# Attention stage of a macaron block: three blocks' normalised rows and the payload's row numbers made on VectorE, and a payload ring of four buffers

## The chip, the cores and the metric

The kernel runs on one core of a Trainium2 chip. TensorE, VectorE, ScalarE, GpSimd and SyncE run their own instruction streams and meet at semaphores. The metric is the device time of one execution in microseconds (us).

## The reference

```python
x = L0_attn_batch                                   # 16 x 512 x 128, float32
x = x + 0.5 * ffn(layernorm(x), ...)                # mixture of 8 experts, 2 per token, and a shared one
x = x + attn(layernorm(x), Wq, bq, Wk, bk, Wv, bv, Wo, bo)
x = x + 0.5 * ffn(layernorm(x), ...)                # the same weights again
# ffn: scores = x @ router; the two best experts of each token, gate = sigmoid(score)
#      out = shared(x) + sum over both experts of (silu(g x @ w_in) * (g x @ w_swiglu)) @ w_out
# attn: softmax over each 128 keys of a sequence of 512 apart, the four results added and normalised
```

## The kernel before

The 8192 tokens are 16 blocks of four tiles of 128 rows. There are five stages: router and shared expert of the first feed-forward layer, its experts, attention, experts again, and an end that adds up. Between stages all engines meet.

**The attention stage** is the one that changes. Each block b goes through it in a hand-written software pipeline: every engine has a loop over i, and the names of helpers with i+3, i, i-2, i-3 tell how far ahead or behind a block is. The order on each engine is the order in the text, and only semaphores tie the engines together.
- SyncE loads the two expert results of each token into `Y2`, two blocks ahead.
- GpSimd adds the two (`total`, L968) and adds the sum to `X` (`added`, L973). It does this for eight blocks at the start, and for the other eight between the scatters of blocks 0 to 7. The scatter of a block (L992) is eight indirect DMAs that write rows of the payload `PAY` to DRAM at the rows in `POS`; their descriptors are made by GpSimd. A payload row is 128 values, the token's result row number (`AT_DEST`) and its gate (`AT_GATE`). Before the scatter GpSimd copies the row numbers (L980) and the second expert's 128 values (L982, in two halves).
- VectorE makes mean and variance (`moments_a`, L1020 and L1024), then, once ScalarE has the inverse deviation `RA`, the product `NA` = -mean x `RA` (`shift`, L1030). It also makes the maxima of the scores (`NM`, L1035), the weights and the scaling of the probabilities (L1058, twice a block, 128x1024), the update of `X` (L1064), the rescaled rows of the payload (`norm`, L1082), the choice of experts (`HOT`, `HOTB`), the gate (`gate`, L1094 and L1096) and the place of each row (`RANK`, `PICK`, `POS`).
- ScalarE makes `RA` (L1167, L1171), the normalised rows `AN` from `X`, `NA` and `RA` (`normalise`, L1178), copies between PSUM and SBUF, and the exponentials (L1215). In its loop `normalise(i + 3)` comes ahead of `exps(i + 1, 0)`.
- TensorE transposes `AN` (L1300), makes queries, keys, values, scores, the products with the values, and transposes the payload's rows once a block (`turn_kept`, L196) for the router.

`AB` is the number of buffers of `PAY` in this stage; block b uses `b % AB`, and `norm` waits for the scatter of block b - AB before it overwrites one.

Of the kernel before, what the change touches and what calls it, by code (L numbers as in the profile page):

```python
# [8 lines left out]
I32 = mybir.dt.int32  # L9
U32 = mybir.dt.uint32  # L10
ACT = mybir.ActivationFunctionType
ALU = mybir.AluOpType
# [3 lines left out]
BT = 4  # L16
# [23 lines left out]
def macaron(nc, batch, wq, bq, wk, bk, wv, bv, wo, bo, router, w_in_sh, w_out_sh, w_sw_sh,  # L40
# [23 lines left out]
    RB = 4  # L64
    AB = 3
    YBUFS = 4
# [11 lines left out]
    with ExitStack() as ctx:  # L78
        def sb(name, shape, dt=F32, mem=ctx):
            return mem.enter_context(nc.sbuf_tensor(name, shape, dt))  # L80
# [841 lines left out]
        with ExitStack() as mem, nc.Block() as block:  # L922
# [26 lines left out]
            KL = sb("KLa", [P, EARLY, W], F32R, mem=mem)  # L949
            SSG = sb("SSGa", [P, FC, W], mem=mem)  # L950
            EARLY_BANKS = ((4, 5), (0, 6))
            HID = Y2[:, :, :, :, :].rearrange("p b c j d -> p b (c j d)")
# [12 lines left out]
            def _(pool):  # L965
# [10 lines left out]
                def second(b, h):  # L976
                    half = slice(h * BT // 2, (h + 1) * BT // 2)
                    if h == 0:
                        pool.wait_ge(k["normed"], NB + b + 1)
                        pool.tensor_copy(PAY[:, b % AB, :, :, AT_DEST:AT_DEST + 1].bitcast(I32),  # L980
                                         dest[:, :, BT * b:BT * b + BT].unsqueeze(3))
                    pool.tensor_copy(PAY[:, b % AB, 1, half, 0:D], PAY[:, b % AB, 0, half, 0:D])\  # L982
                        .then_inc(k["pay2"], 1)
# [29 lines left out]
            def _(dve):  # L1013
# [13 lines left out]
                def shift(b):  # L1027

                    dve.wait_ge(k["a_rstd"], b + 1)
                    dve.scalar_tensor_tensor(out=NA[:, b % 4, :], in0=MA[:, b % 4, :, 0], scalar=-1.0, in1=RA[:, b % 4, :],  # L1030
                                             op0=ALU.mult, op1=ALU.mult).then_inc(k["a_shift"], 1)
# [60 lines left out]
                def gate(b):  # L1092
                    dve.wait_ge(k["gate_raw"], NB + b + 1)
                    st.did(dve.tensor_scalar(GE[:, b % 2, :, :], GE[:, b % 2, :, :], 1.0, None, ALU.add))  # L1094
                    st.settle()
                    dve.reciprocal(PAY[:, b % AB, :, :, AT_GATE:AT_GATE + 1],  # L1096
                                   GE[:, b % 2, :, :].rearrange("p j c -> p c j").unsqueeze(3)).then_inc(k["gated"], 1)
# [64 lines left out]
            def _(act):  # L1162
# [10 lines left out]
                def normalise(b):  # L1173
                    act.wait_ge(k["a_shift"], b + 1)
                    if b >= 2:
# [348 lines left out]
```

## Time and profile before

| | |
|---|---|
| three runs | 991.25 us median (988.44 to 995.65) |
| the profiled execution | 990.6 us, of which the profile's span is 988.9 us |
| attention's first sum on GpSimd | starts at 418.90 us |
| last sum of `X` on GpSimd (L973) | starts at 592.56 us |
| last scatter DMA issued by GpSimd (L992) | starts at 701.93 us, takes 0.96 us |
| last VectorE operation of attention | starts at 702.52 us, takes 0.69 us |
| first loads of the next stage on SyncE's queue | 707.45 us |
| busy over the span | PE 84%, DVE 65%, ACT 58%, POOL 65% |

Times in rows are from the start of the span. PE is TensorE, DVE VectorE, ACT ScalarE, POOL GpSimd, SP SyncE. A time stands for the whole stage only where the stage's rows say so; the shares over the span are means over stages with different limits.

### The profile page before, as it was taken

Reading aid. Unit: us, or ns where it says so; the run is one execution under the profiler, and the core shown is the slowest. Engines: PE = TensorE matmul, PEld = TensorE weight load, DVE = VectorE, ACT = ScalarE, POOL = GpSimd, SP = SyncE. Lnnn points to the kernel's source line nnn. Section 1 sums busy time; section 2 is a strip of 40 time slices with the busy share of each in tenths; the row PEclk is TensorE's granted clock in tenths of the full one; section 3 lists DMA queues with packets and bytes.
Section 4 is the critical chain, followed back from the end, with each engine's and each line's share of the span. In section 5 each row is a group of like instructions: output and inputs, shape, how many; then the busy total and the mean of one; then the engine's idle time right before and its main releaser. Section 6 shows DMA issues by size and latency. Waiting matters only on the chain. (4 is left out here: it accounts for less than half of the span.)

```text
span 988.9 us, 19495 instructions
## 1 busy us (share of the span) xinstructions
PE 835.5 (84%) x5857; PEld 732.3 (74%) x5857; DVE 644.2 (65%) x2022; ACT 573.3 (58%) x1662; POOL 647.2 (65%) x701
## 2 busy tenths in 40 slices
PE   4787777609999999369999999996599999994997
PEld 3676666509999999326776767775499999993886
DVE  6786654506666666157899998885366666661666
ACT  3324232117777777279988888862277777772332
POOL 4777777745777777470688887677367777774421
PEclk9797777959999999779999999996699999997999
DMA  9611111422333333250112211112423333333653
GB/s 233 189 47 44 44 46 43 85 70 71 104 106 102 109 107 102 74 150 22 49 59 75 79 39 40 36 44 63 88 80 103 109 106 109 101 97 109 170 153 105
DMA packets 112920, 88.01 MB, mean 89 GB/s; under 512 B 13426, under 2 KB 102132, under 8 KB 112820
## 3 DMA queue, kind: packets, MB, share of 16 engines
q1 hardware_dynamic: 94816, 51.08, 20.6%
q0 software_dynamic: 17280, 35.69, 10.8%
q8 instruction: 51, 0.84, 0.4%
q14 instruction: 49, 0.40, 0.1%
q10 hardware_dynamic: 724, 0.01, 0.0%
HBM read 43.68 MB, written 43.04 MB: 88 GB/s over the span
## 5 line engine op out<-in xcount | busy, mean ns | idle before, releaser
L820 POOL DMA_INDIRECT results<-YO,XS x284 | 275.6, 970 | 120.5 <-issue 84.7
L802 DVE TENSOR_TENSOR HT<-bank,SG 128x512 f32<-128x512 f32 x142 | 98.1, 691 | 132.9 <-PE bank L888 132.9
L886 PE MATMUL bank<-XSH,WX 128*128 128x256 f32 x568 | 174.1, 306 | 0.3 <-DVE WX L811 0.3
L992 POOL DMA_INDIRECT pairs<-PAY,POS x128 | 134.8, 1053 | 59.0 <-issue 28.8
L411 POOL DMA_INDIRECT pairs<-PAY,POS x128 | 128.3, 1002 | 57.8 <-issue 30.8
L887 PE MATMUL bank<-XSL,WX 128*128 128x256 f32 x568 | 162.0, 285 | 0.0
L888 PE MATMUL bank<-XSH,WX 128*128 128x256 f32 x568 | 161.9, 285 | 0.0
L904 PE MATMUL bank<-WOE,HT 128*128 x1136 | 150.2, 275 | 0.1
L904 PEld LDWEIGHTS bank<-WOE,HT 128*128 128x128 f32 x1136 | 138.1, 192 | 0.5 <-issue 0.5
L844 ACT ACTIVATE XG<-XS 128x128 f32<-128x128 f32 x284 | 111.0, 392 | 44.1 <-DMA XS<-pairs 44.1
L863 ACT ACTIVATE SG<-bank 128x512 f32<-128x512 f32 x142 | 84.9, 598 | 48.8 <-PE bank L888 48.8
L886 PEld LDWEIGHTS bank<-XSH,WX 128*128 128x128 f32 x568 | 110.2, 194 | 1.1 <-issue 1.1
L887 PEld LDWEIGHTS bank<-XSL,WX 128*128 128x128 f32 x568 | 110.7, 195 | 0.0
L888 PEld LDWEIGHTS bank<-XSH,WX 128*128 128x128 f32 x568 | 110.1, 194 | 0.0
L811 DVE CAST WX<-WE 128x1024 fp32r x142 | 97.4, 686 | 0.1
L1215 ACT ACTIVATE PR<-bank,NM 128x128 f32<-128x128 f32 x256 | 90.6, 378 | 1.0 <-DVE NM L1035 1.0
L894 PE MATMUL bank<-ident,XG 128*128 128x128 f32 x284 | 55.8, 279 | 35.0 <-ACT XG L844 35.0
L456 ACT ACTIVATE SSG<-bank 128x512 f32<-128x512 f32 x32 | 19.1, 595 | 113.7 <-PE bank L636 113.7
L808 DVE TENSOR_TENSOR XSL<-bank,XSH 128x256 fp32r<-128x256 f32 x142 | 58.7, 414 | 35.3 <-ACT XSH L849 35.2
L855 ACT ACTIVATE YO<-bank 128x256 f32<-128x256 f32 x142 | 54.7, 385 | 36.4 <-PE bank L904 36.4
L1363 PEld LDWEIGHTS bank<-V,PT 128*128 128x128 f32 x512 | 63.9, 197 | 6.7 <-issue 6.7
L1339 PE MATMUL bank<-KT,QT 128*128 128x512 f32 x128 | 65.7, 596 | 3.0 <-ACT PR L1215 2.5
(197 smaller groups left out, 1760.9 us busy)
## 6 DMA issues: line engine op xcount, KB each, us to landing
XS<-pairs SPq DMA_DIRECT2D x142, 130.0 KB, 2.3
Y<-results SPq DMA_DIRECT2D x32, 256.0 KB, 3.3
YF<-results SPq DMA_DIRECT2D x32, 256.0 KB, 3.4
results<-YO,XS POOLq DMA_INDIRECT x284
pairs<-PAY,POS POOLq DMA_INDIRECT x256, 2.3
out<-X SPq DMA_DIRECT2D x16, 256.0 KB, 2.5
pairs<-pad_rows SPq DMA_DIRECT2D x16, 130.0 KB
pairs<-pad_rows SPq DMA_DIRECT2D x1, 1040.0 KB, 15.3
```

What stands on the lines that cost most here:

```text
L411: pool.indirect_dma_start(pairs, bass.IndirectOffsetOnAxis(ap=POS[:, b % RB, j, c:c + 1], axis=0), PAY[:, b % RB, c, j, :], None).then_inc ...
L802: dve.tensor_tensor(HT[:, i % 2, :], bank[4 + i % 2][:, :], SG[:, i % 2, :], ALU.mult)\
L811: dve.tensor_copy(WX[:, i % 2, :, :].rearrange("p h f -> p (h f)"), WE[:, ds(e * 4 * F, 4 * F)]).then_inc(k["e_weights"], 1)
L820: pool.indirect_dma_start(results, bass.IndirectOffsetOnAxis(ap=XS[:, u, j, AT_DEST:AT_DEST + 1].bitcast(U32), axis=0), YO[:, u, j, :], No ...
L844: act.activation(XG[:, i % 2, j, :], XS[:, slot(i), j, 0:D], ACT.Copy, scale=XS[:, slot(i), j, AT_GATE:AT_GATE + 1]).then_inc(k["xs_scaled ...
L863: act.activation(SG[:, i % 2, :], bank[2 + i % 2][:, :], ACT.Silu).then_inc(k["e_silu"], 1)
L886: pe.matmul(ps, WX[:, i % 2, 1, w], hi, start=True, stop=False)
L887: pe.matmul(ps, WX[:, i % 2, 0, w], lo, start=False, stop=False)
L888: mm = pe.matmul(ps, WX[:, i % 2, 0, w], hi, start=False, stop=True)
L904: mm = pe.matmul(chunk(bank[6 + i % 2], j), HT[:, i % 2, (2 * c + j) * P:(2 * c + j + 1) * P], WOE[:, ds(e * FC * D + c * D, D)], start=(c ...
L992: pool.indirect_dma_start(pairs, bass.IndirectOffsetOnAxis(ap=POS[:, b % AB, j, c:c + 1], axis=0), PAY[:, b % AB, c, j, :], None).then_inc ...
L1215: ins = act.activation(PR[:, b % 2, a, g * P:(g + 1) * P], chunk(bank[4 + a % 2], g), ACT.Exp, bias=NM[:, b % 2, a, g:g + 1], accum_out=SU ...
```

## The change

`AB` goes from 3 to 4. For the first three blocks VectorE makes the normalised rows itself, in four instructions of one 128x128 tile each, in the place where it made `NA`; ScalarE leaves these three blocks out. The copy of the row numbers into the payload goes from GpSimd's `second` to VectorE's `gate`, in all 16 blocks.

```diff
-    AB = 3
+    AB = 4
...
+            FIRST = 3
...
                     if h == 0:
                         pool.wait_ge(k["normed"], NB + b + 1)
-                        pool.tensor_copy(PAY[:, b % AB, :, :, AT_DEST:AT_DEST + 1].bitcast(I32),
-                                         dest[:, :, BT * b:BT * b + BT].unsqueeze(3))
...
                 def shift(b):
-
                     dve.wait_ge(k["a_rstd"], b + 1)
+                    if b < FIRST:
+                        if b >= 2:
+                            dve.wait_ge(k["a_turned"], b - 1)
+                        for j in range(BT):
+                            ins = dve.tensor_scalar(AN[:, b % 2, j:j + 1, :], x_tile(b, j), MA[:, b % 4, j, 0:1],
+                                                    RA[:, b % 4, j:j + 1], ALU.subtract, ALU.mult)
+                        ins.then_inc(k["a_normed"], 1)
+                        return
...
                     st.settle()
+                    dve.tensor_copy(PAY[:, b % AB, :, :, AT_DEST:AT_DEST + 1].bitcast(I32),
+                                    dest[:, :, BT * b:BT * b + BT].unsqueeze(3))
                     dve.reciprocal(PAY[:, b % AB, :, :, AT_GATE:AT_GATE + 1],
...
                 def normalise(b):
-                    act.wait_ge(k["a_shift"], b + 1)
+                    if b < FIRST:
+                        return
+                    act.wait_ge(k["a_shift"], b + 1 - FIRST)
```

VectorE at the start of attention, before (`SA` and `MA` are the moments of a block, `NM` the first maximum of block 0's scores):

```order
L1020 BN_STATS SA<-X 128x6 x4
L1024 BN_AGGR MA<-SA 128x2 x4
L1030 SCALAR_TENSOR_TENSOR NA<-MA,RA 128x4
L1020 BN_STATS SA<-X 128x6 x4
L1024 BN_AGGR MA<-SA 128x2 x4
L1030 SCALAR_TENSOR_TENSOR NA<-MA,RA 128x4
L1020 BN_STATS SA<-X 128x6 x4
L1024 BN_AGGR MA<-SA 128x2 x4
L1030 SCALAR_TENSOR_TENSOR NA<-MA,RA 128x4
L1035 TENSOR_REDUCE NM<-bank 128x4
```

and now:

```order
L1019 BN_STATS SA<-X 128x6 x4
L1023 BN_AGGR MA<-SA 128x2 x4
L1032 TENSOR_SCALAR AN<-X,MA,RA 128x128 x4
L1019 BN_STATS SA<-X 128x6 x4
L1023 BN_AGGR MA<-SA 128x2 x4
L1032 TENSOR_SCALAR AN<-X,MA,RA 128x128 x4
L1019 BN_STATS SA<-X 128x6 x4
L1023 BN_AGGR MA<-SA 128x2 x4
L1032 TENSOR_SCALAR AN<-X,MA,RA 128x128 x4
L1041 TENSOR_REDUCE NM<-bank 128x4
```

Four instructions of a whole tile stand in the place of each product of 128x4, ahead of the next block's moments and of the first maximum.

GpSimd around the payload of the second block, before:

```order
L973 TENSOR_TENSOR X<-X,Y 128x512
L992 DMA pairs<-PAY,POS 69632x130 x2
L980 COPY PAY<-dest 128x8
L982 COPY PAY<-PAY 128x2x128
L992 DMA pairs<-PAY,POS 69632x130 x2
L968 TENSOR_TENSOR Y<-Y 128x512
```

and now:

```order
L974 TENSOR_TENSOR X<-X,Y 128x512
L991 DMA pairs<-PAY,POS 69632x130 x2
L981 COPY PAY<-PAY 128x2x128
L991 DMA pairs<-PAY,POS 69632x130 x2
L969 TENSOR_TENSOR Y<-Y 128x512
```

The copy of the row numbers is gone, and the copy of the values stands directly behind the last scatter of the block before. VectorE around the gate of a block, now:

```order
L221 TENSOR_TENSOR HOT<-TOPI,expert_no 128x64
L226 TENSOR_TENSOR HOTB<-HOT 128x32
L1100 TENSOR_SCALAR GE<-GE 128x8
L1102 COPY PAY<-dest 128x8
L1104 RECIPROCAL PAY<-GE 128x8
L1041 TENSOR_REDUCE NM<-bank 128x4
L230 TENSOR_TENSOR RANK<-bank,next_row 128x32
```

The copy (L1102) is new in this row; the others stood there in the same order.

## Rows read from the trace of the kernel before

**Rows 1.** Busy time by stretch; columns: stretch, its length, each engine's busy time.

```profile
core 0: us, PE busy (x) PEld busy (x) DVE busy (x) ACT busy (x) POOL busy (x), PEclk, DMA share, GB/s
432.00:447.00 15.00, 12.48 (x37) 5.42 (x38) 10.01 (x30) 14.61 (x59) 9.87 (x8) 1.00 0.58 168
...
493.00:599.00 106.00, 102.88 (x654) 75.42 (x655) 101.29 (x377) 90.19 (x348) 87.46 (x91) 1.00 0.20 61
```

**Rows 2.** Timeline of TensorE, one operation a block; columns: start, duration, engine, line.

```profile
480.94 0.49 PE L196 MATMUL bank<-ident,PAY 128*128 128x128 f32 x3
...
602.34 0.38 PE L196 MATMUL bank<-ident,PAY 128*128 128x128 f32 x2
...
616.96 0.27 PE L196 MATMUL bank<-ident,PAY 128*128 128x128 f32 x1
```

**Rows 3.** Timeline of VectorE and GpSimd in a block at 535 us.

```profile
534.63 1.47 DVE L1058 TENSOR_TENSOR PR<-PR,WG 128x1024 f32<-128x1024 f32 x1
535.13 1.02 POOL L980 COPY PAY<-dest 128x8 int32<-128x8 int32 x1
...
538.81 2.88 DVE L1082 TENSOR_SCALAR PAY<-X,MR,RR 128x128 f32<-128x128 f32 x4
539.56 1.27 POOL L968 TENSOR_TENSOR Y<-Y 128x512 f32<-128x512 f32 x1
```

**Rows 4.** Timeline of VectorE in a block without sums.

```profile
614.56 1.11 DVE L1082 TENSOR_SCALAR PAY<-X,MR,RR 128x128 f32<-128x128 f32 x4
```

**Rows 5.** Timeline of VectorE and GpSimd between 483 and 490 us.

```profile
483.21 1.22 DVE L1058 TENSOR_TENSOR PR<-PR,WG 128x1024 f32<-128x1024 f32 x1
483.50 1.78 POOL L992 DMA_INDIRECT pairs<-PAY,POS  x1 [0.30 <-issue]
...
488.29 0.19 DVE L230 TENSOR_TENSOR RANK<-bank,next_row 128x32 f32<-128x32 f32 x1 [0.36 <-PE bank L190]
...
489.00 0.21 POOL L980 COPY PAY<-dest 128x8 int32<-128x8 int32 x1
...
489.13 1.48 POOL L982 COPY PAY<-PAY 128x256 f32<-128x256 f32 x1
489.14 1.22 DVE L1058 TENSOR_TENSOR PR<-PR,WG 128x1024 f32<-128x1024 f32 x1
```

**Rows 6.** Timeline of VectorE and GpSimd at two later meetings.

```profile
651.64 0.39 POOL L982 COPY PAY<-PAY 128x256 f32<-128x256 f32 x1
...
651.82 1.29 DVE L1058 TENSOR_TENSOR PR<-PR,WG 128x1024 f32<-128x1024 f32 x1
...
690.28 0.73 DVE L272 TENSOR_TENSOR tbl<-tile_no,tcnt 1x576 f32<-1x576 f32 x1
690.32 0.95 POOL L982 COPY PAY<-PAY 128x256 f32<-128x256 f32 x1
```

**Rows 7.** Instructions of line 517, first stage; durations in ns: least, median, most.

```profile
L517 DVE COPY PAY<-dest x16: 165/168/368, 15.8 to 176.9; 128x8 int32<-128x8 int32 x16
```

**Rows 8.** Instructions of line 1030; the same columns.

```profile
L1030 DVE SCALAR_TENSOR_TENSOR NA<-MA,RA x16: 147/152/776, 423.5 to 615.6; 128x4 f32<-128x4 f32 x16
```

**Rows 9.** Timeline at the start of attention.

```profile
426.22 0.41 DVE L1030 SCALAR_TENSOR_TENSOR NA<-MA,RA 128x4 f32<-128x4 f32 x1 [0.84 <-ACT RA L1171]
426.68 1.27 POOL L973 TENSOR_TENSOR X<-X,Y 128x512 f32<-128x512 f32 x1
...
432.24 0.78 DVE L1030 SCALAR_TENSOR_TENSOR NA<-MA,RA 128x4 f32<-128x4 f32 x1 [2.97 <-ACT RA L1171]
433.05 1.65 ACT L1178 ACTIVATE AN<-X,NA,RA 128x128 f32<-128x128 f32 x4 [0.36 <-DVE NA L1030]
433.07 0.69 DVE L1035 TENSOR_REDUCE NM<-bank 128x4 f32<-128x512 f32 x1
...
434.61 0.34 ACT L1215 ACTIVATE PR<-bank,NM 128x128 f32<-128x128 f32 x1
```

**Rows 10.** Timeline of VectorE and GpSimd in the first stage.

```profile
29.53 1.25 DVE L511 TENSOR_SCALAR PAY<-X,MV,RST 128x128 f32<-128x128 f32 x4
...
29.70 0.49 POOL L404 COPY PAY<-PAY 128x256 f32<-128x256 f32 x1
```

## The prediction

> **What bounds the kernel now.** I read the table by stretch first, since the change touches the attention stage alone. Between 493 and 599 us TensorE, busy for 102.88 of 106 us, has 3.1 us of holes although its work is all there, and VectorE is busy for 101.29 us [rows 1]. Then I took TensorE's transpose of the kept rows, which runs once a block, as a clock of the stage: from 602.34 to 616.96 a block takes 14.62 us, but from 480.94 to 602.34 eight blocks take 121.40 us, 15.18 each [rows 2]. At 14.62 they would take 116.96. So 4.44 us are lost in these eight blocks, and the reader is to see why.
>
> The timeline of VectorE and GpSimd in one such block shows it [rows 3]. VectorE's four rescalings of rows (L1082) take 2.88 us there, and 1.11 us at 614.56, when GpSimd has no sums left [rows 4]. They begin at 538.81, and GpSimd's sum L968 (539.56, 1.27 us) ends at 540.83; what is left after 540.83 is 0.86 us, the length of the four without their first wait. So VectorE is held until GpSimd's sum is over. The reverse stands there too: GpSimd's copy L980 takes 1.02 us where it takes 0.21 elsewhere [rows 5], and ends at 536.15, just behind VectorE's product L1058 (534.63 to 536.10). The block is then a ring of two pieces: GpSimd from the end of L1058 to the end of its next L968 (536.10 to 540.83, 4.73 us), then VectorE from there to the end of its next L1058, which is the rest of the 15.18, about 10.5 us. Each engine waits for the other once a block, in SBUF access and not at a semaphore, so the view of waits does not list it.
>
> The ring closes in the block before 493 us [rows 5]. GpSimd comes to L980 at 489.00 and gets through it in 0.21 us; its next copy, L982, starts at 489.13, VectorE's L1058 at 489.14, and L982 takes 1.48 us instead of 0.39 [rows 5, 6]. From there GpSimd is more than a microsecond late, its L968 falls on L1082, and the ring holds to the end of the sums.
>
> The Trainium skill says on "SBUF — State Buffer", section "Who interferes with whom", that VectorE and GpSimd share one pair of ports, held for the whole instruction, and that the one that issues first blocks the other. The stalls agree with it; taken at its word, L982 with its start 0.01 us ahead should have won, and the row shows that it lost.
>
> **Part 1, the payload's row numbers go from GpSimd to VectorE.** Taken off GpSimd: one L980 a block, 0.13 us from start to start where nothing holds it (489.00 to 489.13). What counts is where it stood: L982 now starts at 489.00, 0.14 us ahead of L1058. Does it win? L980 at that very start was not held (0.21 us), and at 651.64 an L982 that starts 0.18 us ahead of L1058 takes its plain 0.39 us while L1058 takes 1.29 instead of 1.22 [rows 5, 6]. A lead of 0.01 loses, leads of 0.14 and 0.18 do not: I take it that L982 wins. Then GpSimd issues its scatter some 1.2 us earlier (489.00 and L982's 0.39 and the steps behind it, instead of 490.61 and the same steps), L968 runs from about 492.6 to 493.9, and L1082 is held for 0.8 us instead of 1.6. The four end near 494.8; TensorE, at its free pace, asks for them at 480.94 + 14.62 = 495.56. The hold is hidden.
>
> Does it stay so? GpSimd's descriptors at 483.50 take 1.78 us and end 0.85 us behind the end of VectorE's first L1058 (483.21 + 1.22) [rows 5], so that GpSimd is set anew in every block from VectorE's own clock, and comes to L982 4.57 us after that end. From the first L1058 to the second VectorE takes 5.93 us at its free pace, so the lead is 5.93 - 1.22 - 4.57 = 0.14 us in each block, and does not drift. What it gives back is 4.44 us: **-4.4**, or nothing if the race is lost (bounds -4.5 and +0.5).
>
> Put on VectorE: 16 copies of 128x8. The same copy is made there in the first stage, at 165 to 368 ns [rows 7]. It is ahead of the gate's reciprocal, and behind that VectorE stands idle for 0.36 us before RANK, waiting for TensorE [rows 5]. In the free pace this idle time covers it: 0. If that cover is gone, as in the ring, it costs up to 0.07 to 0.2 us a block, against which L982, now first behind L1058, ends about 0.1 us sooner than L980 and L982 together: about 0, within 1 us over eight blocks.
>
> **Part 2, VectorE makes the rows of blocks 0 to 2.** ScalarE loses three times 1.65 us, VectorE gets three times the 1.11 us of the same form and loses three small products [rows 4, 9]. But here GpSimd makes its sums nearly back to back, and the small product NA already waits for them: 0.41 us at 426.22 and 0.78 at 432.24, where the operation takes 0.15 [rows 8, 9]. The rows are four instructions, and two engines that both want SBUF alternate: in the first stage a GpSimd copy at 29.70 gets in between four such instructions, which then take 1.25 us [rows 10].
> Block 0: NA's hold is the same, the rows end near 424.9 instead of 425.8, but ScalarE's next step needs the moments of block 1, which VectorE makes only behind the rows. Gain 0.3 at most.
> Block 1: the scale is ready at about 426.7, just as L973 starts (426.68). One instruction behind it, one or two behind the next L968, the last behind L973: ready at about 430.9, which is when TensorE used to take them.
> Block 2 decides. The moments come 2.8 us later than before, after the rows of block 1; the scale is ready at about 432.7; the rows wait for L968 (to 433.02, as NA does) and for one L973 between them, and end at 434.8. Behind them in VectorE's queue stands the first maximum, NM, which was made at 433.07, and behind that ScalarE's first exponentials, which began at 434.61 after ScalarE's own rows. Now NM ends at about 435.5, and so the exponentials start 0.9 us later. ScalarE is busy for 14.61 of 15 us from 432 on [rows 1], so this lag runs through the stage. Value **+0.9**. From below: if the rows met no sums, ScalarE would start on NM's end at 433.8, -0.8, and with block 0's 0.3 about -1.1. From above: two more sums of 1.27 between the four, +3.5.
>
> **Part 3, four buffers.** L1082 would wait for a scatter three blocks old; no row shows VectorE idle before it for that reason, its length in the free stretch is the plain 1.11 us [rows 4], and in the ring it is explained by L968 to within 0.03 us. With four, nothing is late next: 0.
>
> **Part 4, the end.** GpSimd's scatters are the last work of the stage (the table of times above), so what GpSimd gains behind its last wait comes out at the end. Its last L982 takes 0.95 us, beside VectorE's table operation, which starts at 690.28, 0.04 us ahead of it, and takes 0.73 [rows 6]. Two L980 less (0.13 each) put it 0.2 us ahead of the operation, and it would end in 0.39: **-0.6**, a cautious share of the 0.26 + 0.56 (from 0, when another hold swallows it, to -1.4, when the next hold is missed too).
>
> **Sum.** -4.4 + 0.9 - 0.6 = -4.1 on the profiled execution's 990.6: 986.5. That execution lies 0.65 below the median of the three runs, so the forecast is 987.1.
>
> **Rivals.**
> 1. The ring stays. L1058 gets hold of SBUF although L982 starts 0.14 us ahead, or the lead shrinks by a tenth of a microsecond through the copy that VectorE now makes. The row for it is L982's loss at a lead of 0.01, and that the threshold lies anywhere up to 0.14. Then -0.4 + 0.9 - 0.6 = -0.1, and the time is 991.2. The Trainium skill, "Perfetto Trace Analysis", section "Optimizing Scalar/DVE Operations", says that moving work between GpSimd and VectorE might not help since they share a port; by that rule the outcome is this one.
> 2. Slower: the start. VectorE's rows of block 2 are cut up by GpSimd's sums, all four one sum apart, and NM and everything behind it start at 438 instead of 434.6. It decides from the point where NM is more than 4 us late, which eats all that the ring gives; with the ring in place as well the time is 990.6 + 3.5 - 0.4 + 0.65 = 994.3. For it speaks that NA met a sum in two blocks out of two shown; against it, that the sums come in pairs with holes while they wait for their loads.
> 3. A better start. The rows slip into a hole, ScalarE's 1.65 us really go: 987.1 - 2.0 = 985.1.
> 4. The change doesn't do what its words say for the time: the payload's fourth buffer is never asked for, part 3. This changes none of the sums.
>
> **How the numbers follow.** Forecast 0.47, ring stays 0.28, start slower with the ring in place 0.10 and with it gone (989.7) 0.07, better start 0.08. The three runs shown reach from 988.44 to 995.65, so about 1% is what a measurement of this kernel can tell from no change, and every case lies inside it: faster by over 1% 0.03, slower by over 1% 0.02. The range goes from 984.0, the forecast with the tail's and the start's better ends in part, to 994.5, rival 2.
>
> **What would show it.** Ring gone: L1082 near 1.1 to 2.0 us instead of 2.7 to 2.9 in all blocks, L982 at 0.4 us, TensorE's transposes 14.6 us apart from 480 on. Part 2: the first exponentials of attention about 0.9 us later than 434.61 as counted from the first sum. Part 4: the last L982 at 0.4 us. The forecast is wrong if L982 still takes over a microsecond in the second block, or if the rows of block 2 take over 3 us.

## The result and the profile after

The kernel with the change takes 995.81 us (median of 20 runs, 990.59 to 1001.18), the kernel before took 991.87 us in the same rounds (20 runs). The ratio is 1.0045, with a 95% interval of 1.0024 to 1.0066: slower by about 4.5 us, where 987.1 was forecast. The profiled execution after took 995.9 us, its span is 994.2 us against 988.9.

The kernel changed in this way was profiled a second time later, under the name after_again. I measure the stages from VectorE's first moments of attention (L1020 before, L1019 after) and read each from the timeline; all numbers are us:

| stretch | before | after | after_again |
|---|---|---|---|
| start of the program to the first moments | 421.61 | 420.00 | 426.72 |
| first moments to the first shift NM | 11.46 | 15.03 | 12.99 |
| first moments to the first exponentials | 13.00 | 15.75 | 13.70 |
| first moments to the first kept transpose (L196) | 44.71 | 50.94 | 45.45 |
| first ten kept transposes, nine distances | 136.02 | 134.39 | 133.97 |
| the other six distances | 78.98 | 76.35 | 78.87 |
| last kept transpose to GpSimd's last scatter | 20.61 | 21.99 | 19.53 |
| attention: first moments to last scatter | 280.32 | 283.67 | 277.81 |
| last scatter to the second experts' first XG | 7.79 | 8.54 | 8.59 |
| from there to the end | 279.2 | 282.0 | 283.3 |

So three things show. The start is late by 6.2 us in one execution and by 0.7 in the other. The stretch of the ring is shorter by 1.6 to 2.1 us, not by 4.4. And 0.8 us went behind the last scatter, in both.

**The start.** After, timeline of all engines between 430 and 445 us (start, duration, engine, line, operation; in square brackets the idle time before and what ended it):

```profile
430.85 4.26 DVE L1032 TENSOR_SCALAR AN<-X,MA,RA 128x128 f32<-128x128 f32 x4 [0.60 <-ACT RA L1179]
431.20 1.27 POOL L974 TENSOR_TENSOR X<-X,Y 128x512 f32<-128x512 f32 x1
432.42 1.27 POOL L969 TENSOR_TENSOR Y<-Y 128x512 f32<-128x512 f32 x1
433.77 1.26 POOL L974 TENSOR_TENSOR X<-X,Y 128x512 f32<-128x512 f32 x1
435.03 0.68 DVE L1041 TENSOR_REDUCE NM<-bank 128x4 f32<-128x512 f32 x1
435.75 0.37 ACT L1225 ACTIVATE PR<-bank,NM 128x128 f32<-128x128 f32 x1 [4.44 <-DVE NM L1041]
...
437.40 1.19 PE L1349 MATMUL bank<-KT,QT 128*128 128x512 f32 x1 [3.60 <-ACT PR L1225]
...
444.76 0.69 DVE L1041 TENSOR_REDUCE NM<-bank 128x4 f32<-128x512 f32 x1 [4.60 <-PE bank L1349]
```

This answers to [rows 9]. The four instructions that make block 2's rows take 4.26 us, because three sums of GpSimd stand among them; with no sum beside them four such instructions take 1.11 [rows 4]. NM is next in VectorE's queue, then ScalarE's exponentials, which end an idle time of 4.44 us, then TensorE's next product, which ends one of 3.60 us. Then the windows of after (stretch, length, busy time and instructions of each engine, granted clock, DMA):

```profile
core 0: us, PE busy (x) PEld busy (x) DVE busy (x) ACT busy (x) POOL busy (x), PEclk, DMA share, GB/s
...
430.00:437.00 7.00, 3.67 (x8) 1.44 (x8) 6.36 (x18) 2.25 (x10) 5.82 (x5) 0.92 0.59 173
437.00:446.00 9.00, 8.60 (x19) 4.55 (x19) 1.93 (x4) 5.81 (x26) 4.11 (x4) 0.50 0.54 156
...
498.00:603.00 105.00, 103.55 (x659) 75.86 (x658) 99.52 (x386) 91.04 (x350) 86.19 (x85) 1.00 0.20 62
```

TensorE, busy for 3.67 of 7 us up to 437, runs at a granted clock of 0.50 (1.2 GHz of 2.4) from 437 to 446. It is busy for 8.60 of 9 us there and does 19 instructions; the mean of 0.92 from 430 to 437 puts the fall of the clock inside its idle time. Before, the clock was 1.00 there and ScalarE the busy engine (14.61 of 15 us, [rows 1]); now ScalarE is busy for 5.81 of 9.

**The ring.** After, timeline of VectorE and GpSimd in the block where it closes and in a later one (to [rows 5] and [rows 3]):

```profile
492.92 0.19 DVE L230 TENSOR_TENSOR RANK<-bank,next_row 128x32 f32<-128x32 f32 x1 [0.36 <-PE bank L190]
...
493.22 0.26 DVE L235 TENSOR_TENSOR PICK<-HOT,RANK 128x64 f32<-128x64 f32 x1
493.64 1.48 POOL L981 COPY PAY<-PAY 128x256 f32<-128x256 f32 x1
493.65 1.22 DVE L1064 TENSOR_TENSOR PR<-PR,WG 128x1024 f32<-128x1024 f32 x1
...
538.64 1.32 DVE L1064 TENSOR_TENSOR PR<-PR,WG 128x1024 f32<-128x1024 f32 x1
539.12 1.09 POOL L981 COPY PAY<-PAY 128x256 f32<-128x256 f32 x1
542.80 2.63 DVE L1088 TENSOR_SCALAR PAY<-X,MR,RR 128x128 f32<-128x128 f32 x4
543.28 1.28 POOL L969 TENSOR_TENSOR Y<-Y 128x512 f32<-128x512 f32 x1
```

GpSimd's payload copy (L982, now L981) again starts 0.01 us ahead of VectorE's product and again takes 1.48 us. Without L980 the copy comes sooner, but the product does too. Before, timeline:

```profile
488.04 0.96 POOL L992 DMA_INDIRECT pairs<-PAY,POS  x1 [0.31 <-issue]
488.60 0.37 DVE L235 TENSOR_TENSOR PICK<-HOT,RANK 128x64 f32<-128x64 f32 x1
```

From RANK's start to the product's it was 0.85 us before (488.29 to 489.14, [rows 5]) and is 0.73 now (492.92 to 493.65), and most of the difference is PICK: 0.37 us then, 0.26 now. What made PICK longer is not shown: by the timeline it had ended at 488.97, 0.03 us ahead of L980's start. The ring that follows is a softer one: the copy 1.09 us, the rows L1088 2.63 us. TensorE's kept transposes, timeline of after (to [rows 2]):

```profile
485.56 0.60 PE L196 MATMUL bank<-ident,PAY 128*128 128x128 f32 x4
...
605.33 0.60 PE L196 MATMUL bank<-ident,PAY 128*128 128x128 f32 x4
619.96 0.60 PE L196 MATMUL bank<-ident,PAY 128*128 128x128 f32 x4
```

Eight blocks take 119.77 us, 14.97 each (15.18 before); a free one takes 14.63.

**Behind the last scatter.** After, timeline:

```profile
703.67 0.96 POOL L991 DMA_INDIRECT pairs<-PAY,POS  x1 [0.30 <-issue]
...
709.93 2.85 SPq L836 DMA_DIRECT2D XS<-pairs  x5
```

6.26 us from the last scatter to the first load of the second experts. Before, in the same view:

```profile
701.93 0.96 POOL L992 DMA_INDIRECT pairs<-PAY,POS  x1 [0.30 <-issue]
...
707.45 2.85 SPq L836 DMA_DIRECT2D XS<-pairs  x5
```

5.52 us.

### The profile page after: what moved, and what is told of

It reads as the page before. It is cut to its first block and busy times, and to the rows that moved or that the text cites. A ratio compares the mean times of both kernels' runs of the same rounds, so it can differ in the third digit from the quotient of the medians.

```text
span 994.2 us, 19492 instructions
## 1 busy us (share of the span) xinstructions
PE 835.8 (84%) x5857; PEld 729.9 (73%) x5857; DVE 651.5 (66%) x2047; ACT 567.7 (57%) x1650; POOL 646.2 (65%) x685
## 5 line engine op out<-in xcount | busy, mean ns | idle before, releaser
L820 POOL DMA_INDIRECT results<-YO,XS x284 | 278.8, 982 | 120.9 <-issue 83.2
L855 ACT ACTIVATE YO<-bank 128x256 f32<-128x256 f32 x142 | 54.6, 384 | 33.3 <-PE bank L904 33.1
L1349 PE MATMUL bank<-KT,QT 128*128 128x512 f32 x128 | 68.0, 617 | 5.4 <-ACT PR L1225 5.0
```

The lines of the kernel that those rows point to most:

```text
L820: pool.indirect_dma_start(results, bass.IndirectOffsetOnAxis(ap=XS[:, u, j, AT_DEST:AT_DEST + 1].bitcast(U32), axis=0), YO[:, u, j, :], No ...
```

## The experiments

Kernels of one job share the runs of the kernel before. The jobs ran on different chips: on those of the first two jobs the kernel before took 992.33 and 991.68 us, on the next two 1066.59 and 1066.46, on the last 1092.28. Only ratios are compared across them. What the expectations call "the ten blocks" are the nine distances of the table.

### One part at a time

rows_only has the rows of blocks 0 to 2 on VectorE and nothing else, copy_only has the copy of the row numbers alone, buffers_only the fourth buffer alone, and rows_two is the whole change with two blocks in place of three:

```diff
-            FIRST = 3
+            FIRST = 2
```

> VectorE makes the rows of blocks 0 to 2, nothing else is changed. Theory A (the rows alternate with GpSimd's sums, the first maximum comes late, TensorE stands idle and its clock falls): counted from VectorE's first moments of attention, the first kept transpose of TensorE comes 5 to 6.5 us later than in the kernel before (44.7 us there), the granted clock is near 0.5 for some 8 us behind a hole of TensorE of over 3 us, and the time is 4 to 6 us above before. Theory B (the loss comes from the moved copy or from the buffers): the first kept transpose comes within 1 us of 44.7, and the time is that of before.

> Only the copy of the row numbers moves to VectorE. Theory A: the start is as before (44.7 us from first moments to first kept transpose), the ring stays, at about 15.03 us a block instead of 15.28, and the time is 1.5 to 2.5 us below before. The prediction's theory (GpSimd's copy wins and the ring goes): 14.62 us a block, 4.4 us below before. Theory B: slower by 2 us or more.

> Only the payload's fourth buffer. Theory A: no difference within what the rounds tell, 15.28 us a block as before. A rival (the fourth buffer lets VectorE run ahead and meet GpSimd elsewhere): another time a block than 15.28.

> The whole change, but VectorE makes the rows of blocks 0 and 1 only, and ScalarE those of block 2 as before. Theory A: it is the third block's rows, ahead of the first maximum, that open the hole; with them back on ScalarE the hole is under 2 us, the clock stays at 1.0, and the first kept transpose is 1 to 2 us behind the 44.7 us of before, the time 3 to 5 us below the full change. If instead block 1's rows are enough to delay everything (its moments come late for block 2), it is 3 us or more behind.

| kernel | ratio to before (95%) | first kept transpose | nine distances | attention |
|---|---|---|---|---|
| rows_only | 1.0048 (1.0016 to 1.0081) | +45.67 | 136.02 | 280.31 |
| copy_only | 1.0010 (0.9975 to 1.0045) | +44.54 | 134.35 | 277.18 |
| buffers_only | 0.9998 (0.9963 to 1.0034) | +44.58 | 136.06 | 279.25 |
| rows_two | 0.9968 (0.9936 to 1.0001) | +44.42 | 133.56 | 276.38 |

The loss belongs to the rows, and within them to the third block: with two blocks nothing is late. What is gained in the nine distances belongs to the copy; alone it gives as much of it as the whole change, and PICK takes 0.25 us in it and the lead is 0.01 us, as after. The 1.5 to 2.5 us that were expected of it are not seen in its timed runs (1.0010), whose interval doesn't exclude them either. And rows_only's profiled execution has its first kept transpose only 0.96 us late and no low clock, although its runs are as slow as those of the change. So either the profile caught an exception, or the loss lies elsewhere.

rows_two also shows what decides the race. Its timeline, GpSimd and VectorE, blocks 2 and 3:

```profile
503.91 0.42 POOL L981 COPY PAY<-PAY 128x256 f32<-128x256 f32 x1
503.94 1.47 DVE L1064 TENSOR_TENSOR PR<-PR,WG 128x1024 f32<-128x1024 f32 x1
...
518.55 1.49 POOL L981 COPY PAY<-PAY 128x256 f32<-128x256 f32 x1
518.56 1.22 DVE L1064 TENSOR_TENSOR PR<-PR,WG 128x1024 f32<-128x1024 f32 x1
```

By the unrounded starts, over the profiles of all kernels, thirteen copies that came 0.008 to 0.021 us ahead lost, and five that came 0.023 to 0.033 us ahead won. The lead that the prediction counted on was not 0.14 us but one to three hundredths.

### Is the late start an accident, and does the clock have a share in it?

after_again is the change once more. filled adds four needless products on TensorE ahead of its wait for the first probabilities:

```diff
+                    if i == -1:
+                        for _ in range(4):
+                            pe.matmul(bank[7][:, :], WT[:, 0, :], AXT[:, 1, :], start=True, stop=True)
```

> The change itself, profiled and timed again, as the neighbour of the next two kernels. Theory A (the start of attention gives back what the ring gives): the first kept transpose again stands about 51 us behind VectorE's first moments, with a stretch at TensorE's 1.2 GHz level (granted clock 0.50) just before it, and the ratio to the kernel before is again near 1.0045. Rival B (the low clock was an accident of the one profiled execution): the clock stays at 1.00 there, the first kept transpose stands 46 to 48 us behind the first moments, and the ratio is nearer to 1.000.

> The change, with four needless 128x512 products on TensorE into a free bank just ahead of its wait for the first probabilities, where it stood idle for 3.60 us. Nothing else differs, and the products leave no result. Theory A (the idle TensorE loses its clock, and products that take 1.06 us in place of 0.60 then pay for the late start a second time): the granted clock is 1.00 between 437 and 446 us, the first kept transpose comes about 3 us sooner than after the change (near +48 us behind the first moments), and the kernel is 2 to 3 us faster than after the change, a ratio to before of about 1.002. Rival B (the start is late only because the shift and the first exponentials are late): the clock changes or not, but the first kept transpose stays within 0.7 us of the change's, and so does the time.

after_again: ratio 1.0028 (0.9997 to 1.0058), and a profile with an early start. Its timeline where block 2's rows are made:

```profile
437.64 2.14 DVE L1032 TENSOR_SCALAR AN<-X,MA,RA 128x128 f32<-128x128 f32 x4 [0.60 <-ACT RA L1179]
437.92 1.27 POOL L974 TENSOR_TENSOR X<-X,Y 128x512 f32<-128x512 f32 x1
...
439.71 0.68 DVE L1041 TENSOR_REDUCE NM<-bank 128x4 f32<-128x512 f32 x1
439.81 1.26 POOL L969 TENSOR_TENSOR Y<-Y 128x512 f32<-128x512 f32 x1 [0.62 <-DMA Y<-results]
```

Here GpSimd's next sum had to wait for its load, so only one sum stands among the four instructions, and they take 2.14 us. The clock stayed at 1.00. That this execution was nevertheless long (998.0 us) comes from the experts: there GpSimd's scatters L820 follow each other at 1.27 us, and in the first experts 25 of the 141 distances were over 1.4 us, in place of one in before and in after; in the second experts 11, as in after, in place of 2 before. In all of these GpSimd waited for no other engine; the scatter itself took 1.1 to 1.5 us in place of 0.97. This varies from execution to execution in code that the change does not touch (in the first experts 12 in rows_only, 7 in rows_two, one in copy_only), and is why single executions don't tell kernels of this kind apart.

filled: 992.44 us, ratio 1.0011 (0.9976 to 1.0045), against 996.13 for after_again in the same job. Its windows:

```profile
437.00:446.00 9.00, 7.65 (x26) 3.45 (x25) 5.34 (x23) 8.97 (x39) 4.78 (x4) 1.00 0.57 167
```

NM at +15.03 and the exponentials at +15.74 are as late as in after, but the clock is 1.00, ScalarE is busy for 8.97 of 9 us, and the first kept transpose comes at +47.50 in place of +50.94. Theory A holds: of the 6.2 us, 3.4 are the low clock, and 2.8 are the late exponentials themselves. The timed runs agree (3.7 us less than after_again), though the intervals of the two ratios overlap.

### The sums give way

yielded is the change with one more wait on GpSimd:

```diff
                 def added(b):
                     pool.wait_ge(k["summed"], b + 1)
+                    if b == 3:
+                        pool.wait_ge(k["a_normed"], 3)
```

> The change, with one more wait on GpSimd: its sum into X for block 3 (L974 of the change's kernel) waits until VectorE has made the rows of block 2. Theory A (the start is late because VectorE makes the rows of block 2 in turns with GpSimd's sums, 4.26 us in the first profiled execution of the change, 2.14 us in the second, where a late load held the sums off): the four instructions now take 1.3 to 1.6 us, the shift of block 0 (NM) comes 12.0 to 12.5 us behind the first moments in place of 15.03, the clock holds 1.00 behind it, the first kept transpose comes at +44.5 to +45.5 in place of +50.94, and the kernel is 4 to 6 us faster than the change, a ratio to before of 0.997 to 0.999. Rival B (the sums that wait are then missing further on, and block 3's moments hold VectorE and the scores instead): the rows of block 2 are quick, but the first kept transpose stays at +48 or later, and the time is that of the change.

Its timeline:

```profile
468.00 1.11 DVE L1034 TENSOR_SCALAR AN<-X,MA,RA 128x128 f32<-128x128 f32 x4 [1.47 <-ACT RA L1181]
469.02 0.69 DVE L1043 TENSOR_REDUCE NM<-bank 128x4 f32<-128x512 f32 x1
469.26 1.26 POOL L976 TENSOR_TENSOR X<-X,Y 128x512 f32<-128x512 f32 x1 [4.53 <-DVE AN L1034]
```

NM at +11.60, first kept transpose at +44.88, ratio 0.9991 (0.9974 to 1.0009). The sum waited 4.53 us, and neither NM nor the first kept transpose was late for it. As this was another chip, the change was run beside it in a further job, with the kernel before profiled as well:

> The kernel before, profiled on the chip of the next three. Both theories expect what its first profile showed: first kept transpose at +44.7 us behind the first moments, the first ten blocks in 136.0 us, attention in 280.3 us, 5.5 us from GpSimd's last scatter to the first load of the second experts. If GpSimd's scatters are slower on this chip, the ten blocks take longer and the next three have to be read against this row.

> The change, timed in the same rounds as the kernel whose GpSimd waits. Theory A (the late start is the rule, and the execution without it was the exception): NM at about +15.0 us, first kept transpose at +50.9, clock 0.50 in a stretch behind it, and a time 4 to 6 us above the kernel whose GpSimd waits, so about 1.003 to 1.005 of the time before. Rival B (the loss lies outside attention, in the experts, where GpSimd's scatters come with more or less of a delay from execution to execution): the start varies between executions and the time is within 2 us of the kernel whose GpSimd waits.

> The change with GpSimd's sum for block 3 waiting for VectorE's rows of block 2, timed in the same rounds as the change. Theory A: NM at about +11.6 us, first kept transpose at +44.9, no low clock behind it, 4 to 6 us faster than the change and 0.997 to 0.999 of the time before. Rival B: the same early start, and a time within 2 us of the change.

after_side 1072.05 us, ratio 1.0050 (1.0021 to 1.0078); yielded_side 1066.55 us, ratio 1.0007 (0.9983 to 1.0032). One wait took away 5.5 us. after_side's start, timeline and windows:

```profile
467.67 4.49 DVE L1032 TENSOR_SCALAR AN<-X,MA,RA 128x128 f32<-128x128 f32 x4 [0.60 <-ACT RA L1179]
```

```profile
474.00:484.00 10.00, 9.04 (x19) 4.55 (x19) 2.46 (x5) 6.81 (x32) 4.26 (x4) 0.51 0.49 142
```

First kept transpose at +51.01, and at +44.07 in yielded_side, +44.81 in before_side. Attention: 287.91, 279.80 and 280.65 us. Theory A holds here: the late start is what the timed runs of this chip carry. On the chips of 992 us the 3.7 us between filled and after_again point the same way, but two of the four profiles there with three blocks' rows on VectorE (after_again, rows_only) have the earlier start, so how often it comes is not known.

before_side brought a surprise: half a ring. VectorE's rows L1082 take 2.7 us in three of the eight blocks with sums and 1.3 to 1.8 in the others, where the first profile had 2.7 to 2.9 in seven; L980 is held (1.07 to 1.10 us) in four, in place of seven; and the nine distances take 133.43 us instead of 136.02. GpSimd's scatters also run otherwise on this chip, as the page shows for the experts, first before, then before_side (line, count, busy time and mean ns, idle time before):

```profile
L820 POOL DMA_INDIRECT results<-YO,XS x284 | 275.6, 970 | 120.5 <-issue 84.7
```

```profile
L820 POOL DMA_INDIRECT results<-YO,XS x284 | 304.8, 1073 | 169.8 <-ACT YO L855 97.5
```

Here 56 of the 141 distances in a stage are over 1.4 us. Two things are in them. In the first experts 33 are longer scatters, up to 1.75 us apart; the other 23, up to 3.3 us, end when ScalarE has written YO (L855), so there GpSimd waits for the engines ahead of it. The idle time in front of the scatters grew by 49 us over both stages, their busy time by 29. The other engines wait as well: between 230 and 400 us TensorE is busy for 150.67 of 170 us, where before it was busy for all 170. What makes these chips slower is not shown. In attention the meetings of copy and product fall elsewhere, so on this chip the ring holds in fewer blocks, and the change (133.64 us) has nothing to gain there.

### The ring: a lead for the copy, or no sums

lead is rows_two with three tiny copies on VectorE behind the row numbers; copy_lead has them in copy_only. sums_ahead is the kernel before with all of GpSimd's sums ahead of its scatters.

```diff
                     dve_place(dve, st, NB + b, b % AB, bank[1])
+                    for n in range(3):
+                        dve.tensor_copy(PADW[:, n, :], WR[:, n, :])
```

```diff
-                for i in range(-8, NB):
+                for i in range(-NB, NB):
...
-                    if 0 <= i + 8 < NB:
-                        total(i + 8)
+                    if 0 <= i + NB < NB:
+                        total(i + NB)
```

> The kernel with two blocks' rows on VectorE, with the copy and the fourth buffer, and with three tiny needless copies on VectorE (about 0.06 us each) behind the row numbers, so that VectorE's second scaling is issued some 0.18 us later than GpSimd's second payload copy, in place of 0.01 us ahead or behind. Theory A (the ring of VectorE and GpSimd hangs on which of the two instructions starts first, by hundredths of a microsecond): every payload copy takes about 0.4 us, the blocks come 14.62 us apart from the second on, where the kernel with two blocks' rows had 15.03 from the fourth, so that the ten blocks take another 1.9 to 2.0 us less (131.6 in place of 133.56), and the ratio to before is 0.993 to 0.995. Rival B (it is not the order of these two, but the sums among GpSimd's scatters that hold the ring): the payload copies still take over a microsecond in most blocks, the distance stays 15.03 or more, and the three copies only add time to VectorE.

> The kernel before, with GpSimd's sums of all sixteen blocks issued ahead of its first scatter, in place of eight ahead and eight among the scatters. Rows and row numbers stay where they were before. Theory A (the ring needs the sums L968 and L973 among the scatters: they push the next payload copy behind VectorE's scaling): the first sums still let the first eight blocks start as before, all sixteen are done before the first scatter or little after it, every payload copy takes about 0.4 us, the blocks come 14.62 us apart and the ten blocks take 131.6 us in place of 136.0, a ratio of about 0.9955. Rival B (the ring holds itself by the payload copy and the scaling alone): the blocks stay 15.0 to 15.3 us apart and the time is that of before or longer, since the sums now lie beside VectorE's first blocks.

> The kernel before with the copy of the row numbers on VectorE alone (rows on ScalarE, three buffers), and three tiny needless copies behind the row numbers that put VectorE's second scaling some 0.18 us later. Theory A (the ring is lost or won by the order of two starts, and GpSimd's own chain, 14.72 us for a block, is what sets the distance once it is won): payload copies of 0.4 us in the first seven or more blocks, the ten blocks in 131.6 to 132.5 us in place of 134.35 for the copy alone and 136.02 before, and a ratio to before of 0.994 to 0.997. Rival B (a gain in attention of this size doesn't reach the end, since the experts behind it run at GpSimd's scatters and start when the last rows are there): the ten blocks are short as in A, but the ratio stays within 0.998 to 1.002.

> The kernel before with the copy of the row numbers and three tiny needless copies on VectorE, in the same rounds. Theory A (what attention gains reaches the end): payload copies of 0.4 us, the ten blocks in about 132 us where the kernel before has 136, and 0.995 to 0.997 of its time. Rival B (GpSimd's scatters behind attention take it back): the ten blocks as short, the ratio 0.998 to 1.001.

lead, ratio 0.9970 (0.9936 to 1.0003). GpSimd and VectorE, timeline:

```profile
560.27 0.41 POOL L982 COPY PAY<-PAY 128x256 f32<-128x256 f32 x1
560.30 0.42 DVE L1110 COPY PADW<-WR 128x4 f32<-128x4 f32 x1
...
560.77 1.21 DVE L1065 TENSOR_TENSOR PR<-PR,WG 128x1024 f32<-128x1024 f32 x1
...
574.99 1.39 POOL L982 COPY PAY<-PAY 128x256 f32<-128x256 f32 x1
```

The copy is now 0.50 us ahead of the product (not 0.18: the first tiny copy, issued 0.03 us behind it, waits for it, 0.42 us), and takes 0.41. The rows that follow in each block take 1.4 to 1.8 us, which is the 1.1 to 2.0 that the prediction gave for a ring that is gone, and seven distances in a row are 14.6 us, where before they were 15.3. Then the race is lost after all: from 560.27 to 574.99 GpSimd's own chain took 14.72 us without a pause, 0.09 us more than a block, so the 0.03 us on the first tiny copy are used up, and the copy starts 0.08 us behind the product. The nine distances are 132.11 us, attention 275.43, the shortest of all. sums_ahead settles it from the other side: copies of 0.39 us and distances of 14.61 in all blocks but the first (15.07), together 131.98. One of its copies, timeline:

```profile
562.02 0.39 POOL L982 COPY PAY<-PAY 128x256 f32<-128x256 f32 x1
```

Its first kept transpose comes 1.6 us late (+46.27), as the sums now lie beside VectorE's first blocks. Theory A holds for both: the ring needs the sums among the scatters and a lost race.

The times follow only in part, and theory A's ratios were missed in all four. lead (0.993 to 0.995 expected) has 1.0 inside its interval. sums_ahead came out at 1.0013 (0.9976 to 1.0051) though its attention is 276.99 us, 3.3 less than before. In the profiles the stretch behind attention took it back: from the second experts' first XG to the end it was 286.2 us in lead and 283.1 in sums_ahead against 279.2 before, with 18 and 11 of the 141 distances of L820 over 1.4 us against 2. buffers_only, whose attention is hardly shorter, has 13 of them, so this need not come from the change; with one profile a kernel it stays open. copy_lead came out at 0.9992 (0.9971 to 1.0012), with nine distances of 132.31 us and no copy held, and copy_lead_side at 1.0007 (0.9988 to 1.0025), both as their rival B has it, on chips where little is to be won: 133.07 us in copy_lead_side against 133.43 in before_side, although the rows take 1.8 us at most in every block.

### The fourth buffer

lead_three is lead with AB = 3. waits_back is lead with GpSimd's last waits turned round:

```diff
-                for n in range(AB):
+                for n in reversed(range(AB)):
                     pool.wait_ge(scattered2[n], SENT * len(range(n, NB, AB)))
```

> The kernel called lead (two blocks' rows, the copy and three tiny copies on VectorE), with three payload buffers in place of four. Theory A (the fourth buffer costs about 0.7 us at the end of attention: from GpSimd's last scatter to the first load of the second experts stood 5.4 to 5.5 us in the four executions with three buffers, 6.1 to 6.2 in those with four, and nothing in attention asks for it): the stretch is 5.4 to 5.5 us, attention is as with four buffers, 275 to 276 us, and the time is 0.7 us less, too little for the timing to show. Rival B (the 0.7 us belongs to something else in those kernels): the stretch is 6.1 us or more.

> The kernel called lead with its four buffers, where GpSimd's last waits, one for each buffer's scatters, stand in the reverse order, so that the buffer of the last block is waited for first and not last. Theory A (the 0.7 us comes from the wait for the last block's buffer standing behind three others): the stretch from the last scatter to the first load of the second experts falls from 6.19 to about 5.5 us. Rival B (it has another cause, such as how many scatters one count has to collect, or where the buffers lie): it stays at 6.1 to 6.2 us, and the cause stays open.

The end of attention in lead_three, and then in waits_back (one run, timeline):

```profile
737.17 0.96 POOL L992 DMA_INDIRECT pairs<-PAY,POS  x1 [0.30 <-issue]
742.75 1.07 SPq L836 DMA_DIRECT2D XS<-pairs  x2
```

```profile
736.17 0.98 POOL L992 DMA_INDIRECT pairs<-PAY,POS  x1 [0.30 <-issue]
742.45 1.77 SPq L836 DMA_DIRECT2D XS<-pairs  x3
```

5.58 us with three buffers, 6.28 with four in either order of the waits. The other executions with three buffers have 5.4 to 5.9 us, but for best_copy (below) with 8.7, and those with four 6.1 to 6.9 (yielded the longest). But for that one execution it goes with the number of buffers; the order of the waits is not the cause, and what is stays open. lead_three's ratio is 0.9989 (0.9970 to 1.0009), on a chip of 1066 us.

### A kernel that beats both

best_rows is lead_three and best_copy is copy_lead, run once more.

> Two blocks' rows and the copy on VectorE, three tiny needless copies behind the row numbers, three payload buffers: the kernel called lead_three once more, for another chip. Theory A (what attention gains reaches the end where GpSimd's scatters in the experts don't set the pace): if the chip is one on which the kernel before takes about 992 us, attention takes 275 to 276 us against 280.3, 5.4 to 5.5 us from the last scatter to the next load, and 0.994 to 0.997 of the time before. On a chip with 1066 us: 0.998 to 1.001. Rival B (the gain is taken back behind attention on either chip): 0.998 or more on both.

> The copy alone on VectorE with the three tiny copies, three payload buffers: the kernel called copy_lead once more. Theory A: as best_rows, within 0.7 us of it in attention, since the rows of two blocks neither gain nor lose at the start (first kept transpose at +44.4 in the one, +44.7 in the other), so 0.994 to 0.997 where the kernel before takes about 992 us and 0.998 to 1.001 where it takes 1066. Rival B: 0.998 or more on both.

The chip was the slowest, with 1092.28 us for the kernel before. best_rows took 1086.51 us, ratio 0.9951 (0.9922 to 0.9980), best_copy 1087.45 us, ratio 0.9960 (0.9932 to 0.9988). Both are faster than the kernel before there, but attention took 281.5 and 281.8 us, not 275 to 276, and the kernel before was not profiled on that chip. That the gain is the ring's is not shown: by theory A a chip with slow scatters should have given 0.998 or more.

## Why the prediction was wrong

**Part 1 (-4.4), the failed step.** The mechanism was right: a ring of VectorE and GpSimd, closed by one lost race of L982 and L1058, kept up by the sums among the scatters. lead and sums_ahead each undid it and gave distances of 14.6 us. The step that failed is "L982 now starts at 489.00, 0.14 us ahead of L1058". It moved one instruction forward and left the other at its old start. Without L980 VectorE's PICK takes 0.26 us in place of 0.37, so the product comes a tenth sooner as well; the lead was 0.01 us again, and the race is lost up to 0.021. The calculation of the lead (5.93 - 1.22 - 4.57 = 0.14) failed with it, since its 5.93 us held the longer PICK; what it rested on held, for before and after every scatter issued during an L1058 (now L1064) ended 0.83 to 0.87 us behind that product's end. Two of the signs that the prediction named for being wrong came true: the copy took 1.48 us in the second block, and block 2's rows 4.26. Rival 1 named the way ("the lead shrinks by a tenth of a microsecond") for another cause. Yet the ring that stayed is 0.25 us a block looser (15.03 against 15.28), which rival 1 priced at -0.4 in all and which measured -1.6 over the nine distances.

The Trainium skill's rule ("SBUF — State Buffer", "Who interferes with whom": the one that issues first blocks the other) holds in the runs for leads of 0.023 us and more, and not for those of 0.008 to 0.021, by the starts that the profile records.

**Part 2 (+0.9), the costlier failure.** It named the right place and order: block 2's rows, NM behind them, ScalarE behind that. Up to the start of block 2's rows its times held within 0.3 us. The term was mis-sized twice. It let one sum stand among the four instructions; there were three when the load behind them was in time (4.26 us, and the exponentials 2.75 us late; 4.49 in after_side), and one only when the load was late (2.14 us, 0.7 late, which is nearly the forecast's 0.9). And it ended with the exponentials. TensorE's idle time of 3.60 us and the granted clock of 0.50 behind it, for 9 us, cost another 3.4 us, as filled shows. The upper bound of +3.5 held the first alone; the whole is +6.2. Rival 2 had the picture ("all four one sum apart", NM late), not the clock. Its "4 us late" was nearly reached: NM came 3.6 us late.

**Part 3 (0)** was right that nothing waits for a buffer: buffers_only changes nothing in the blocks, and its time is that of before. But the count of buffers has a price outside the blocks, 0.7 us behind the last scatter, for which the profile of before has no row.

**Part 4 (-0.6).** The copy that took 0.95 us is the first half of the last block's and not "its last L982", which took 0.45. It takes 0.41 now, as foretold, but not by a lead of 0.2 us over the table operation. After, timeline:

```profile
691.57 0.73 DVE L272 TENSOR_TENSOR tbl<-tile_no,tcnt 1x576 f32<-1x576 f32 x1
...
693.14 0.41 POOL L981 COPY PAY<-PAY 128x256 f32<-128x256 f32 x1
```

The table operation is over long before the copy starts. In rows_only and buffers_only, where GpSimd still has both L980, that copy takes 0.40 and 0.39 us too. So the number came out by luck. From the tenth kept transpose to the last scatter it is 98.3 us after and 99.6 before, 1.3 less; but rows_only and buffers_only have 98.6 and copy_only 98.3, so 0.3 of it, about two L980 of 0.13, is what the moved copy gives, and the other 1.0 comes without it.

**Sum.** Forecast -4.1. Measured in the profiled execution: -1.6 for program start to first moments, +6.2 start of attention, -1.6 ring, -1.3 end of attention, +0.8 behind the last scatter, +2.8 in the experts and behind: +5.3. The first and the last vary between executions of one kernel. The middle four make +4.1; with only 0.3 of the end of attention put down to the change they make +5.1. The timed ratio (+4.5 us, 2.4 to 6.5) agrees with either. The forecast of "within 1%" held, its range of 984.0 to 994.5 did not. The upper end was rival 2 with the ring in place, 994.3, which leaves out part 4's -0.6, while its other case, 989.7, has it in; neither has a term for the clock or for the stretch behind the last scatter.

## What to carry to other kernels

Where two engines meet within some hundredths of a microsecond, don't forecast the winner: an instruction that is taken away moves both of them, so put some tiny instructions ahead of the one that must lose (three here: the copy won in every block of copy_lead, and in lead in six blocks before it lost), or take the other engine's long instructions out of the loop. Work moved to an engine that shares SBUF with another's long run of instructions is paid at the other's instruction length, once for each instruction; count those that will be ready, not those in the trace, where they may have waited for a load. And price a late start by what it does to TensorE too: an idle time there is paid once as time and a second time if the clock falls.

## What the runs showed of the hardware

- Four VectorE instructions of 0.33 us beside a run of GpSimd sums of 1.27 us take turns with them: 1.11 us for the four when GpSimd waits (yielded), 2.14 and 2.28 with one sum among them (after_again, rows_only), 4.25 to 4.49 with three (after, filled, after_side).
- GpSimd's copy of 128x256 and VectorE's product of 128x1024: if the copy is issued 0.008 to 0.021 us ahead it loses and takes 1.48 us, 0.023 to 0.033 us ahead it wins and takes 0.41 to 0.42, and then the product takes 1.47 to 1.48.
- In an idle time of 3.60 us on TensorE the granted clock fell to 0.50 (1.2 GHz) and was 0.50 over the next 9 us; after_side has the same with 3.54 us of idle time. Four needless products in that idle time (filled) kept it at 1.00 and brought the work behind it 3.4 us forward.
- A GpSimd scatter issued while VectorE is in its product of 128x1024 ends 0.83 to 0.87 us behind the product's end (18 of 18 in before, 18 of 18 in after), and takes up to 1.90 us in place of 0.96.
- The same kernel took 991 to 1092 us on different chips. In the experts the distances of 1.27 us between GpSimd's scatters became 1.4 to 3.5 us in some 40% of the cases on three of the chips, in part through longer scatters, for the greater part because GpSimd waited for ScalarE; where that starts is open. A ring of two engines that holds in seven blocks on one chip held in three on another.
